# Local attention: where ScalarE takes the squares of the keys within a slot

## The reference, cut to what matters

```
def attn_layer(x, Wqkv, qs, ksc, Wo):
    q, k, v = jnp.split(x @ Wqkv, 3, -1)        # then by heads
    q = l2norm(q) * qs
    k = l2norm(k) * ksc
    q = q * cos * scale + rotate_half(q) * sin * scale
    k = k * cos * inv + rotate_half(k) * sin * inv
    out = local_attention(q, k, v)              # softmax(8 q k^T, masked) v
    return out.transpose(0, 2, 1, 3).reshape(b, n, INNER) @ Wo
```

## Time and profile before

| | us |
|---|---|
| median of 3 runs | 3862.86 |
| lowest, highest | 3859.14, 3867.37 |
| span of the profiled execution | 3862.6 |
| TensorE busy in it | 3675.0 |
| VectorE | 3134.3 |
| ScalarE | 2886.4 |
| GpSimd | 2453.8 |

### The profile page before, as it was taken

One profiled execution on the slowest core, in us unless ns is written; L12 is line 12 of the kernel. 1 busy time (PEld: TensorE's weight loads), 2 busy tenths in 40 slices (PEclk: granted clock), 3 DMA queues, 4 the chain that ended last, 5 costly groups with the idle time before them and its releaser, 6 DMA issues. The chain is left out here.

```text
span 3862.6 us, 189335 instructions
## 1 busy us (share of the span) xinstructions
PE 3675.0 (95%) x70910; PEld 2943.1 (76%) x70910; DVE 3134.3 (81%) x9407; ACT 2886.4 (75%) x8517; POOL 2453.8 (64%) x2556
## 2 busy tenths in 40 slices
PE   7869999999999999999999999999999999899997
PEld 4558888688886788876888868888688886466665
DVE  7878888688887788877888878888788887666667
ACT  5758888478885688866888758888478885677775
POOL 3657777377774677755777647777377773454553
PEclk8979999999999999999999999999999999899998
DMA  1013333233332233332333323333233331100000
GB/s 48 1 56 83 81 82 81 60 81 81 81 81 69 72 81 80 82 83 58 83 80 82 90 52 81 81 81 82 60 81 81 81 81 46 36 1 0 0 0 28
DMA packets 305289, 245.99 MB, mean 64 GB/s; under 512 B 74485, under 2 KB 299860, under 8 KB 304340
## 3 DMA queue, kind: packets, MB, share of 16 engines
q1 hardware_dynamic: 305108, 243.72, 25.0%
HBM read 24.54 MB, written 2.12 MB: 7 GB/s over the span
## 5 line engine op out<-in xcount | busy, mean ns | idle before, releaser
L1233 POOL TENSOR_TENSOR wa_t<-wa_t,wa_rn 128x512 f32<-128x512 f32 x768 | 785.4, 1043 | 280.5 <-DVE wa_rn L1061 277.0
L893 ACT ACTIVATE wa_pb<-wa_sc,wa_nm 128x64 f32<-128x64 f32 x3072 | 672.5, 330 | 365.1 <-DVE wa_nm L1083 340.1
L1239 POOL TENSOR_TENSOR wa_t<-wa_t 128x512 f32<-128x512 f32 x384 | 496.1, 1292 | 409.7 <-DVE wa_t L1037 409.6
L1035 DVE TENSOR_TENSOR wa_t<-wa_pj,wa_ctab 128x512 f32<-128x512 f32 x768 | 527.0, 686 | 210.5 <-PE wa_ta L637 137.6
L45 PE MATMUL wa_pj<-lw_wqkv_high,wa_xhigh 128*128 128x512 f32 x1152 | 532.7, 462 | 36.3 <-DVE wa_t L1037 17.7
L876 ACT ACTIVATE wa_sq<-wa_pj 128x512 f32<-128x512 f32 x768 | 487.5, 636 | 60.4 <-PE wa_pj L47 57.8
L1248 POOL TENSOR_TENSOR wa_t<-wa_t 128x512 f32<-128x512 f32 x384 | 490.1, 1276 | 0.0
L47 PE MATMUL wa_pj<-lw_wqkv_high,wa_xlow 128*128 128x512 f32 x1152 | 459.9, 399 | 0.0
L46 PE MATMUL wa_pj<-lw_wqkv_low,wa_xhigh 128*128 128x512 f32 x1152 | 457.6, 397 | 0.9 <-issue 0.9
L1043 DVE TENSOR_REDUCE wa_raw<-wa_sq 128x16 f32<-128x1024 f32 x384 | 448.9, 1169 | 0.0
L696 PE MATMUL wa_ob<-wa_oT,lw_wo 128*128 128x128 f32 x3120 | 419.7, 278 | 2.7 <-DVE wa_on L1095 2.6
(11 more groups left out here) (291 smaller groups left out, 8631.5 us busy)
## 6 DMA issues: line engine op xcount, KB each, us to landing
wa_vv<-wa_vt SPq DMA_DIRECT2D x2304, 65.0 KB
wa_vv<-wa_vt SPq DMA_DIRECT2D x1152, 32.5 KB
lw_wqkv<-L_ffn_Wqkv SPq DMA_DIRECT2D x6, 1536.0 KB, 6.2
lw_xs<-yT SPq DMA_DIRECT2D x96, 64.0 KB
lw_fs<-yT SPq DMA_DIRECT2D x48, 128.0 KB
lw_xs<-yT SPq DMA_DIRECT2D x96, 63.8 KB
lw_fs<-yT SPq DMA_DIRECT2D x96, 63.8 KB
lw_wo<-L_ffn_Wo SPq DMA_DIRECT2D x6, 512.0 KB, 4.1
```

The costliest lines, as they stand in the source:

```text
L893: last = nc.scalar.activation(pb[:, u.par(2), p, e, :], SC[:, e, p * KEYS:(p + 1) * KEYS], ACT.Exp, bias=nm[:, u.par(2), e, p:p + 1])
L1035: nc.vector.tensor_tensor(t1[:, b, j], x, table(ctab, slice(0, HD)), ALU.mult)
L1233: nc.gpsimd.tensor_tensor(here, here, rn[:, u.par(1), j * HG:(j + 1) * HG].unsqueeze(2).broadcast_to((128, HG, HD)), ALU.mult).then_inc(s. ...
L1239: nc.gpsimd.tensor_tensor(t1[:, b, 0], t1[:, b, 0], t2[:, b, 0], ALU.add).then_inc(s.qadd_done, 1)
```

## The change

ScalarE's `slot` takes the squares of k directly behind the squares of q, in front of the copies of kT and qT. Before, they stood behind these copies. Nothing else is touched; no instruction is added or taken out.

```diff
                     if u.has(0):
                         squares(u, 0)
+                        squares(u, 1)
                     if u.has(2):
                         act.wait_ge(s.qk_done, u.count(2, 2, 1))
...
                         nc.scalar.activation(qT[:, u.par(2), :, :], TA[:, :].rearrange(
                             "p (a b) -> p a b", a=PR), ACT.Copy).then_inc(s.qk_out, 1)
-                    if u.has(0):
-                        squares(u, 1)
```

## The result

The changed kernel takes 3979.23 us (median of 4 runs, 3977.53 to 3984.9) against 3864.08 us for the kernel before (4 runs): a ratio of 1.0303, with a 95% interval of 1.0287 to 1.0318. It is slower by 115 us. The profiled execution spans 3975.9 us against 3862.6, 113 us more.

The account below looks back on a forecast made before the run. The bound was TensorE's own work, with ScalarE's copies nearly level in a closed loop. 360 slots at 0.355 us (127.8) plus 0.6 for the fill, put on 3862.9, gave 3991 us; range 3940 to 4040.

Parts of the forecast that it names:

- rival 1: In local attention TensorE stays the bound and hides the 0.48 us delay of the copies: 3863 us; chance 4%.
- (a): On ScalarE, kT and qT start later by one square's pitch, 0.48 us.
- (b), (c): On ScalarE the moved square waits for nothing new; behind it only pT comes later, as it waits for pb's transposes.
- (d): VectorE's rotation of k gets its square 0.96 us sooner but is held by other work: gain put at nothing.
- Both ways round: From the score start to the squares of q, through the exponentials or, in slot 3, through TensorE's q projection.
- Nor does the delay shrink on the way round: From scores through maximum and exponentials to the next squares of q, nothing of the delay is given back.
- Rival 2: Other parts of the loop give something back: 0.21 us a slot or less, 3939 down to 3925 us; chance 10%.
- The bare wait of 0.71 us: With TensorE waiting, 0.71 us pass from a copy's end to the end of the four transposes, read in the fill.
- spare time: Delay of qT that TensorE hides before the block on TA: 0.06, 0.07, 0.27 and 0.10 us in four slots.
- Rival 3: Every local attention slot pays the full 0.48 us pitch, with 0.05 of wake-up: 4036 to 4054 us; chance 15%.
- Rival 4: VectorE's rotation of k waits for its squares; freeing it wins at most 0.09 us a slot: 3830 us; chance 2%.
- Rival 5: TensorE idles in every local attention slot and the granted clock falls, at 0.97 costing 75 us: 4066 us; chance 3%.

Follow-up runs that it names:

- The dose runs: Kernel before with extra squares in front of kT: one of 64 columns 3870.89 us, one of 512 columns 3988.97 us, two of 512 columns 4151.15 us.

## Why the prediction was right, point by point

- **What bounds the kernel.** The prediction read a loop in which ScalarE's copies are as late as TensorE can just bear. The dose runs show that the first 0.1 us is nearly free and the rest is not, and the kernel before with seven exponentials shows that TensorE's own work is the floor. The reading by occupancy, rival 1 (3863), fell: an engine at 85% cost 3% by its order alone. The Trainium skill, "Perfetto Trace Analysis", section "Identifying the Most-Contended Engine", says to optimize the engine with the highest occupancy first. Of the row of before, with TensorE judged by its weight loads (87.35), that engine is VectorE (89.34), and ScalarE (85.47) comes third, not second as the prediction had it. No run relieved VectorE or TensorE. For ScalarE the rule holds one way, as less work on it brings nothing (0.9998 with seven exponentials), but not the way that rival 1 took it: a worse order on it cost 3%.
- **(a) The pitch.** Right: the row of copies keeps 0.48 us.
- **(b), (c)** Right: the moved square waits for nothing new (both squares run in one row), and pT waits for TensorE instead.
- **(d) The rotation of k.** The gain of early squares was put at nothing; no run isolates it. What lies beneath is seen only with an extra square in front: when the squares of k are late by a further 0.48 us, VectorE does feel it.
- **What sets the end.** The prediction let qT alone set it, by 0.05 us in slot 2, and put kT's block at nothing. For the block on TA this holds: the run with the squares between the copies has the same 0.756 us behind the end of qT. Its 98 us leave 17 of the 115, and 11 of these lie in slower scores, which the prediction didn't foresee.
- **How the loop closes.** Both ways round stand in the prediction. The run with seven exponentials shows a margin of only 0.06 us between the two. "Nor does the delay shrink on the way round" is the step that failed: the maximum follows the scores 0.032 us sooner than before, the squares of q the exponentials 0.033 sooner, and the scores the block on TA 0.020 sooner, 0.085 us a slot or 31 us that the prediction had at nothing. Rival 2 named such a giving back, of the maximum above all, though the time stayed far above its 3939. What makes each of the three stretches shorter wasn't tried.
- **The size.** Forecast 128 us, measured 115 (113 in the profile), the term being 0.355 us a slot. The four slots of the sum grew from 6.575 to 6.918, by 0.343, near it. Over all loaded slots between 6.2 and 7.6 us (367 before, 363 after) the mean from copy to copy of qT is 6.60 before and 6.91 after, 0.31 more; 0.31 x 360 = 112. Two terms were mis-sized, in opposite directions. The bare wait of 0.71 us, taken from the block on TB in the fill, is 0.757 on the mean for the block on TA in the loaded slots, where most read 0.77, so that the true spare time is 0.844 - 0.757 = 0.087 and not 0.125. With the 0.016 us by which qT itself reads longer, 0.404 us a slot pass through the block and not 0.355, 18 us too little in the forecast. The 31 us of the way round were too much. That the sum came out within 13 us is in part luck.
- **Slots are not alike.** A slot that is long before for another reason has more spare time: in the 68 of the 353 slots with 6.65 us or more from scores to scores the distance from the end of qT to the end of the block on TA is 0.919 us on the mean, in the others 0.826.
- **Where it isn't.** The stretches outside the copies' 63 intervals a layer (closing, the gated layers, most of the tail) have 2 us of the 113. The first fill slot hides the delay as forecast: in the first layer its v projection follows an idle time of 1.44 us before and after. In the second, the scores follow those of the first by 6.64 us instead of 6.36, so 0.28 us are exposed and not 0.1, some 2 us in six layers if the others are like it.
- **The signs.** Slots near 6.93 us, the row square, square, kT, qT, the idle time in front of the transposes, the busy times of three engines and the clock came as announced. TensorE's share of the stretch did not: 97.97 and not about 95%; blocks that waited read longer, so part of the waiting is counted as busy.
- **Rivals.** Rival 3 (full pitch, 4036) is what the step from one extra square to two comes near to; for the first square the spare time counts. Rival 4 (faster) fell with the sign of the result. Rival 5 fell: the granted clock stayed 1.00 in the stretch although TensorE idles in each slot.

## What to carry to other kernels

When one engine reads out banks that another waits to fill again, its order is worth what lies between the end of each copy and the moment when the bank is wanted, and not what its busy share leaves free: find places in the trace where the wait is bare, measure it there, and subtract. Work that nobody waits for soon belongs behind the copies, where it cost nothing, and not in front of them, where each 0.1 us beyond the spare time cost 32 to 34 us over 360 slots. Take the bare wait from the loop itself if you can: the one from the fill was 0.05 us short. And don't put the rest of the loop at nothing: here it gave back 0.085 of the 0.475 us.

## What the runs showed of the hardware

An activation's pitch depends on more than its columns. The extra square of 64 columns took 0.103 us of ScalarE's time from start to start (median), one of 512 columns 0.477, which makes 0.374 us for 448 columns, 0.83 ns each. An exponential of 64 columns with a bias took 0.197, 0.094 us more than the square of as many columns. Whether the bias or the function makes this difference wasn't tried. The recorded duration of the small square, 0.28 us, says little: 0.18 of it lie beside kT, which starts 0.10 behind it.

From the end of a copy on ScalarE to the end of four waiting transposes on TensorE it is not always the same: 0.71 us in some slots of the changed kernel, 0.77 in most (medians 0.71 for k = 0 and 0.77 for k = 1, 2 and 3, qT's copy to the block on TA). What makes the difference isn't shown.
